# One fused vision block on one core: the experts of two of its four chunks over 512 tokens instead of 256, and several steps moved

## The reference

```
xe = xn * ln_g[e] + ln_b[e]
h  = gelu(xe @ W1[e] + b1[e])      # 64 -> 256
y  = h @ W2[e] + b2[e]             # 256 -> 64
out = sum over the two chosen experts of weight * y
```

## Time and profile before

| | us |
|---|---|
| median of 3 runs (lowest, highest) | 318.96 (318.73, 320.15) |
| the profiled execution | 318.64 |
| its span | 316.9 |
| busy: TensorE, ScalarE, VectorE, GpSimd | 279.8, 256.5, 242.5, 119.8 |
| mean granted clock of TensorE | 0.981 |

### The profile page before, as it was taken

The page is one execution under the profiler, slowest core; times in us unless marked ns, Lnnn a source line. Parts: engine busy times, 40 slices in busy tenths (PEclk is TensorE's granted clock), DMA queues, the critical chain, the costliest instruction groups (busy, mean ns, idle before and its releaser), DMA issues.

```text
span 316.9 us, 8774 instructions
## 1 busy us (share of the span) xinstructions
PE 279.8 (88%) x3434; PEld 191.4 (60%) x3434; DVE 242.5 (77%) x720; ACT 256.5 (81%) x490; POOL 119.8 (38%) x124
## 2 busy tenths in 40 slices
PE   7976998868799898799899999799879999988894
PEld 2552566645467575476577665576667787766462
DVE  6999769799958999659588997586956453589474
ACT  2587678899897999997988899988949898877562
POOL 5040042405142604054466240090836644279130
PEclk9999799989999999999999999999979999999998
DMA  7910000000000000000000000000000000000000
GB/s 157 289 34 0 2 3 4 2 0 0 2 2 4 3 2 2 0 2 8 3 11 2 2 2 0 3 3 8 2 10 2 1 2 2 10 1 11 2 0 17
DMA packets 7190, 4.86 MB, mean 15 GB/s; under 512 B 5089, under 2 KB 6830, under 8 KB 7086
## 3 DMA queue, kind: packets, MB, share of 16 engines
q1 hardware_dynamic: 7150, 4.31, 5.4%
HBM read 2.04 MB, written 0.52 MB: 8 GB/s over the span
## 4 chain that ended last, share of the span: by engine, by line
PE 38%; DVE 27%; ACT 15%; POOL 11%; issue 8%; DMA 1%; SPq 0%; DVEq 0%; ACTq 0%; POOLq 0%
DVE prod L833 4%; PE m_ps L1583 4%; ACT wk L1256 4%; PE zl_ps L1472 4%; PE zh_ps L1469 3%; ACT wk L1251 3%; PE ga_ps L1503 3%; PE ga_ps L1505 3%; PE ga_ps L1504 3%; POOL lx L531 3%; POOL prod L522 3%; PE m_ps L1564 2%; PE m_ps L1566 2%; DVE samp L848 2%; PE m_ps L1447 1%
## 5 line engine op out<-in xcount | busy, mean ns | idle before, releaser
L833 DVE TENSOR_TENSOR prod<-ga_ps,wx 128x480 f32<-128x480 f32 x96 | 61.8, 650 | 36.0 <-PE ga_ps L1505 35.8
L522 POOL TENSOR_TENSOR prod<-prod 128x960 f32<-128x960 f32 (+1 forms) x20 | 39.4, 1969 | 128.2 <-DVE prod L833 128.2
L1503 PE MATMUL ga_ps<-v_all,wk 128*128 128x80 f16 x576 | 80.5, 204 | 6.2 <-DVE prod L833 5.8
L1251 ACT ACTIVATE wk<-zh_ps 128x512 f16<-128x512 f32 x108 | 65.2, 603 | 20.6 <-PE zh_ps L1469 19.5
L1505 PE MATMUL ga_ps<-v_all,wk 128*128 128x80 f16 x576 | 80.5, 204 | 0.0
L1504 PE MATMUL ga_ps<-v_all,wk 128*128 128x80 f16 x576 | 80.5, 204 | 0.0
L1503 PEld LDWEIGHTS ga_ps<-v_all,wk 128*128 128x128 f16 x576 | 57.5, 100 | 18.4 <-issue 9.5
L1256 ACT ACTIVATE wk<-zl_ps 128x512 f16<-128x512 f32 x108 | 65.0, 602 | 0.0
L1504 PEld LDWEIGHTS ga_ps<-v_all,wk 128*128 128x128 f16 x576 | 57.9, 101 | 6.9 <-issue 0.6
L1505 PEld LDWEIGHTS ga_ps<-v_all,wk 128*128 128x128 f16 x576 | 58.1, 101 | 0.0
L1469 PE MATMUL zh_ps<-tab,sel_hi 128*128 128x512 f16 x108 | 42.4, 393 | 6.8 <-ACT wk L1251 5.5
(11 more groups left out here) (278 smaller groups left out, 592.4 us busy)
## 6 DMA issues: line engine op xcount, KB each, us to landing
v_all<-still SPq DMA_DIRECT2D x1, 1440.0 KB, 9.8
h_all<-in_W SPq DMA_DIRECT2D x1, 512.0 KB
w_s<-in_W SPq DMA_DIRECT2D x1, 512.0 KB
x_tok<-in_x SPq DMA_DIRECT2D x1, 384.0 KB, 4.1
out_dram<-x_tok SPq DMA_DIRECT2D x6, 64.0 KB, 1.6
w_high<-w_high SPq DMA_DIRECT2D x1, 256.0 KB, 2.9
const<-in_table SPq DMA_DIRECT2D x1, 218.0 KB, 2.5
vec<-in_vectors SPq DMA_DIRECT2D x1, 132.5 KB
```

The costliest lines, as they stand in the source:

```text
L522: then(pool.tensor_tensor(p[:, 0:3, :], p[:, 0:3, :], p[:, 3:6, :], ALU.add))
L833: dve.tensor_tensor(prod[q % 2][:].rearrange("p k n -> p (k n)")[:, f * PB * NV:(f + 1) * PB * NV] .rearrange("p (n c l) -> p n c l", n=PB ...
L1251: act.activation(wk[n % WR][:, 0, :], zh_ps[:], ACT.Relu, scale=W_SCALE).then_inc(s_wkh, 1)
L1503: pe.matmul(to, w_h, high, start=True, stop=False)
```

## The change

- Experts of chunks 0 and 1 (`d < LAST - 1`): a unit is one half of the hidden layer of one expert over all 512 tokens, two products of 512 columns. `expert_out` works on a pair of experts over 512 columns, four calls instead of eight. `outputs_out` is four copies of 512 columns. Both halves are transposed after all experts are done, the second into `m_ps[0]` and `m_ps[1]`; `input_t` and `samples_t` of later chunks wait for `s_y_rd` for that reason. Chunks 2 and 3 keep the old form.
- `x2` has two buffers, so `residual` waits for the chunk before the last.
- `offsets` signals `s_om` after each bank, `positions` waits for each.
- `input_stats(1)` stands after `hats(0)` instead of before `positions(0)`.
- Products of zeros: two after each of the two first tables, two each at places 19, 19 and 20.5 of the first chunk and at 0 and 3 of the last.
- `outputs_last`: the last 256 tokens by 16 multiply-adds of 64 columns in two chains.
- The tables of places are new. Those that the prediction speaks of are in the diff; others move by a unit or a few.

```diff
 PE_FIRST
-            "bias_product": [0, 0, 0, 3.5, 4.5, 4.5, 5.5, 5.5]}
+            "bias_product": [0, 0, 0, 0, 4.5, 4.5, 5.5, 5.5], "zeros": [19, 20.5, 19]}
...
 PE_MIDDLE
-             "expert_in": [11, 13, 13.5, 14.5, 16.5, 18.5, 19.5, 21, 23, 24, 25.5, 26, 28, 29, 30, 31],
-             "expert_out": [17.5, 19, 20, 23, 27.5, 29.5, 30.5, 32.5], "outputs_t": [25.5, 35.5], "b2": 35}
+             "expert_in": [12, 13, 13.5, 13.5, 16.5, 16.5, 18.5, 18.5, 19.5, 21, 22.5, 23, 24.5, 25, 27, 28],
+             "expert_out": [17.5, 21.5, 26, 31.5], "outputs_t": [32.5, 33], "b2": 35}
...
 ACT_MIDDLE
-              "hidden": [12.5, 12.5, 14.5, 15.5, 18.5, 19, 19.5, 21.5, 24.5, 25, 25.5, 26.5, 28.5, 29.5, 30.5, 31.5],
-              "outputs_out": [23.5, 32.5]}
+              "hidden": [12.5, 12.5, 14.5, 15, 17.5, 18, 18.5, 19.5, 21.5, 22, 22.5, 23.5, 25.5, 26.5, 27.5, 28.5],
+              "outputs_out": [20, 30.5, 30.5, 31.5]}
...
 DVE_MIDDLE
-              "bias_rows": 4.5, "router_parts": 12.5, "w1_low": [8, 9.5, 11, 17], "outputs_in": [23.5, 35]}
+              "router_parts": 12.5, "w1_low": [8, 9.5, 11, 17], "outputs_in": [31.5, 33]}
-POOL_MIDDLE = {"tap_tree": [16.5, 22.5, 25.5, 34.5], "combine": [27, 35.5], "conv_rstd": 21, "inner_rstd": 14,
+POOL_MIDDLE = {"tap_tree": [18.5, 21, 23.5, 35.5], "combine": [35, 35.5], "conv_rstd": 19, "inner_rstd": 12,
...
-POOL_LAST = {"tap_tree": [4, 19.5, 21.5, 35, 42.5, 53.5, 66.5, 71.5], "combine": [37, 53.5], "conv_rstd": 30.5,
-             "inner_rstd": 2.5, "input_rstd": 47, "half_inner_rstd": 44.5, "router_exp": 17.5, "half_router_exp": 71}
+POOL_LAST = {"tap_tree": [4, 21.5, 30.5, 35, 44.5, 55.5, 68, 71.5], "combine": [32.5, 58.5], "conv_rstd": 30.5,
+             "inner_rstd": 0.5, "input_rstd": 47, "half_inner_rstd": 45.5, "router_exp": 25, "half_router_exp": 69.5}
...
@@ positions
-                dve.wait_ge(s_om, a + 1)
-                for t in range(TP):
+                for bank in range(2):
+                    dve.wait_ge(s_om, 2 * a + bank + 1)
+                    for t in range(2 * bank, 2 * bank + 2):
...
@@ outputs_last
+                acc = [seen["wexp"]] * 2
+                parts = [(m_ps[2], m_ps[3], 0, 4), (z_ps[0][:, 0:P], z_ps[0][:, P:2 * P], 4, 2), (ga_ps[0][:, 0:P], ga_ps[0][:, P:2 * P], 6, 2)]
+                for part, (left, right, e0, count) in enumerate(parts):
+                    dve.wait_ge(s_yt, 2 * d + 3 + part)
+                    for e in range(count):
+                        for t, bank in enumerate((left, right)):
+                            dve.wait_ge(s_chain, acc[t])
+                            first, final = e0 + e == 0, e0 + e == E - 1
+                            ins = dve.scalar_tensor_tensor(
+                                out_s[:, d * TP + 2 + t, :] if final else ysum[:, t, :], bank[:, e * C:(e + 1) * C],
+                                wexp[:, 2 + t, e0 + e:e0 + e + 1], x2(d)[:, 2 + t, :] if first else ysum[:, t, :], ALU.mult, ALU.add)
...
@@ vector, start
-            input_stats(1)
             positions(0)
...
             hats(0)
+            dve.wait_ge(s_x_rest, N_X)
+            input_stats(1)
             tap_weights(0)
@@ expert_in
+                if d < LAST - 1:
+                    c0 = n * P
+                    pe.matmul(m_ps[n % 2], w1_high[:, c0:c0 + P], zn_both[:], start=True, stop=False)
+                    pe.matmul(m_ps[n % 2], w1_low[:, c0:c0 + P], zn_high[:], start=False, stop=True).then_inc(s_h, 1)
+                    return
@@ expert_out
+                pe.wait_ge(s_ht, d * (2 * E) + 4 * m + 4)
+                if m == 0:
+                    pe.wait_ge(s_es, min(d + 3, CHUNKS))
+                    pe.wait_ge(s_y_rd, 2 * d)
+                else:
+                    pe.wait_ge(s_ysb, copies_before(d) + m - 1)
+                for a in range(HC):
+                    for r in range(2):
+                        ins = pe.matmul(m_ps[2 + m % 2][r * C:(r + 1) * C, :], w2_s[:, (2 * m + r) * HC + a, :],
+                                        h_t[(4 * m + 2 * r + a) % HR].rearrange("p a n -> p (a n)"), start=(a == 0), stop=(a == HC - 1))
@@ tensor, start
             for r in range(2):
                 features_t(0, r)
+                keep_clock(ga_ps[0][:], FILL[6])
```

More of the change, by code:

```diff
@@ new lines @@
+ACT_FIRST = {"pad_image": 4, "project_high": 8.5, "image_out": 10.5, "conv_gelu": 14.5, "tap_exp": 19.5, "distances": 22.5,
+             "samples_out": 6, "zn_out": 17, "router_exp": 8,
+             "hidden": [4.5, 15.5, 26.5, 34, 34.5, 39, 46.5, 51, 60, 61, 63, 69.5, 69.5, 70, 70.5, 78],
+             "outputs_out": [31.5, 31]}
+DVE_FIRST = {"input_stats": 15.5, "input_norm": 29.5, "input_low": 3.5, "conv_stats": 10, "project_low": 7.5,
+             "conv_norm": 13, "image_out": 13, "positions": [15, 17.5, 15], "rows": [17.5, 17.5, 17.5, 22], "edges": 20.5,
+             "hats": 23.5, "tap_weights": [24.5, 26], "lane_sum": [9.5, 9.5, 17.5, 17.5, 28, 29, 3, 4.5], "residual": 4.5,
+             "inner_norm": 12, "zn_low": 2, "route": [4, 13, 14.5], "expert_weights": 14.5, "b2": 18.5, "bias_rows": 4,
+             "router_parts": 2.5, "w1_low": [7, 8, 14, 26.5], "outputs_in": [17.5, 9.5], "second_stats_": 4,
+             "second_norm": 0.5}
@@ new lines @@
+POOL_FIRST = {"tap_tree": [4, 7, 23.5, 28.5], "combine": [35.5, 22.5], "conv_rstd": 4, "inner_rstd": 21.5,
+              "input_rstd": 26.5}
+PE_MIDDLE = {"input_t": 0, "convolve": [4, 6, 6, 7], "project": 5, "image_t": [9, 12.5], "conv_t": 14.5, "offsets": 15.5,
+             "table": [34, 35.5], "samples_t": 3, "project_out": 4, "experts_t": 8, "router": 11.5,
+             "expert_in": [12, 13, 13.5, 13.5, 16.5, 16.5, 18.5, 18.5, 19.5, 21, 22.5, 23, 24.5, 25, 27, 28],
+             "expert_out": [17.5, 21.5, 26, 31.5], "outputs_t": [32.5, 33], "b2": 35}
@@ L910, in inner_norm @@
                 dve.wait_ge(s_y_r, d + 1 + (half or 0))
[L911 removed]
+                normalise(zn, x2(d), y_mv, y_r[:, 0, :], s_zn, half)
             def logit_scale(d, half=None):
@@ L1351, in body @@
                                 hidden(j - 1, u)
+                        for m in range(E // 2):
+                            if j < LAST and n == at["outputs_out"][m]:
+                                outputs_out(j - 1, m)
                         for i in range(2):
-                            if n == at["outputs_out"][i]:
-                                outputs_out(j - 1, i)
+                            if j == LAST and n == at["outputs_out"][i]:
+                                outputs_out_half(LAST - 1, i)
             act.wait_ge(s_wa, N_WA)
@@ L1574, in expert_out @@
                 if m == 0:
-                    pe.wait_ge(s_es, chunks)
-                    if d == LAST:
-                        pe.wait_ge(s_y_rd, 2 * d)
-                if 2 * m == E and d < CHUNKS - 1:
+                    pe.wait_ge(s_es, CHUNKS)
+                    pe.wait_ge(s_y_rd, 2 * d)
+                if 2 * m == E and d < LAST:
                     pe.wait_ge(s_y_rd, 2 * d + 1)
```

202 lines of the change are left out of this document (104 added, 98 removed).

## The result

The changed kernel takes 322.52 us (median of 4 runs, 320.18 to 324.41) against 318.85 for the kernel before in the same comparison: ratio 1.0121, 95% interval 1.0073 to 1.0170. It is slower by 1.2%. The forecast was 314.7 us and faster, with a chance of 0.77, and its range ended at 318.5. What came is in the main rival (b), which had 0.09: the end of a chunk. The profiled execution took 321.14 us, its span 319.4, at a mean granted clock of 0.989.

The account below looks back on a forecast made before the run. No engine was full; ScalarE and TensorE, handing work over through single banks, were taken to bound it. Terms -0.6 - 0.9 - 0.8 - 1.0 - 0.7 = -4.0 from 318.64 gave 314.7 us on balance, range 311.0 to 318.5.

Parts of the forecast that it names:

- rival (b): Chunk ends: combine ahead of the last tap sum delays the next chunk, 3 us per boundary, 320.7 us; chance 0.09.
- Start-up, -0.6: Before the first tables: moving the moments and signalling offsets by bank together save 0.6 us.
- the cap: First chunk's start: column weights come 0.4 us later, hidden unless TensorE is much earlier; limits the first chunk's gain.
- First chunk, -0.9: First chunk: avoided clock falls gain 1.2 and 0.1 us, uncovered zero products cost 0.4.
- The fall at 31.8: First chunk: TensorE's half clock for 3.4 us vanishes with chance 0.65, helped by four zero products; 1.2 us gained.
- Middle chunks, -0.8: Second and third chunk: 512-token form saves 0.7 us each, longer blocks cost 0.3; net 0.4 each.
- Rival (a): Middle chunks: long bare blocks and end transposes turn the gain into +0.9 us a chunk, 317.3 us; chance 0.20.
- Last chunk, -1.0: Last chunk: GpSimd's power behind the tap sum saves 0.7 us; the clock fall 0.5 less 0.2 for zero products.
- The wait of 3.21 us: Last chunk: VectorE idles behind GpSimd's power and tap sum; removing this gains 0.7 us.
- The fall at 233.2: Last chunk: lowered TensorE clock loses about 1.0 us; even odds that zero products remove it, counted as 0.5.
- Tail, -0.7: End of kernel: last sums as 16 multiply-adds in two chains, 0.20 us apart, finish 0.7 us earlier.
- Rival (c): First and last chunk: zero products catch no clock fall, gains of 1.2 and 0.5 go, 316.4 us; chance 0.12.

Follow-up runs that it names:

- e9_best: e6_before_first with the moments ahead of the positions again, as in the kernel before; 316.21 us, ratio 0.9952.
- e1_two_yb: The changed kernel with two buffers yb instead of one; 324.51 us, ratio 1.0197.
- e8_start_tail: The kernel before with three edits: moments behind the hats, offsets signalled by bank, last sums as multiply-adds; 317.23 us, ratio 0.9971.
- e4_tail_only: The kernel before with only the last sums as 16 multiply-adds; 317.97 us, ratio 0.9978.
- e6_before_first: Changed kernel with two yb, both combines behind the last tap sum, first-chunk tables of before, no zero products in start-up and first chunk; 317.66 us, ratio 0.9980.
- e10_last_tables: e9_best with the last chunk's tables of before and no zero products in that chunk; 315.86 us, ratio 0.9942.
- e7_no_zeros: Changed kernel with two yb and both combines behind the last tap sum, without any new zero products; 319.57 us, ratio 1.0024.
- e3_all_but_512: Kernel before with the change's start-up edits, first-chunk tables, their zero products and last sums, without the 512-token form; 319.52 us, ratio 1.0016.
- e11_block_later: e9_best with the first second-layer block of the middle chunks at place 19 instead of 17.5; 322.45 us, ratio 1.0146.
- e5_order_alone: The changed kernel with its single yb, both combines moved behind the last tap sum; 335.42 us, ratio 1.0535.

## Why the prediction was wrong, point by point

The step that failed is the one put as rival (b): "GpSimd takes the first combine in front of the last tap sum". It was seen, its chain was named and 3 us a boundary was its price, but it got 0.09 where it should have led. The sum put the boundary at nothing. It cost 3.8 us in all: after against e9_best, the difference goes from +0.2 at 1/34 to +3.4 at 2/3, is +3.0 at 3/0, and reaches +4.0 at 3/71 (the first boundary 2.8, the second 1.0). Two things in it were misjudged.

- **The argument against it read a row wrongly.** The tap sum's 3.57 us was taken as a sign of slack. It is a conflict: it started at 155.20, 0.16 behind VectorE's `wx` (the last row below, all of the kernel before), and without a `wx` beside it the same addition takes 2.21 us (158.19 in the rows above), 1.36 less. In the changed kernel it is the combine that starts beside `wx` and takes 2.61 for 1.27, 1.34 more. So the conflict did not go with the new order, it moved to the combine, and what was counted as slack was never given back. The Trainium skill, "SBUF — State Buffer", section "SBUF: two separate sides", says that a VectorE operation with two inputs in SBUF and a GpSimd operation that reads SBUF exclude each other: who starts first holds the shared ports for the whole instruction, and the other is blocked. The traces agree: `wx` reads two tiles in SBUF, starts at 153.58, the combine at 153.75, when 1.48 us of `wx` are left, and the excess is 1.34. They show the other direction too, where GpSimd is in front: VectorE's instruction at 75.67 ends only with the addition that began at 74.54, after 1.72 us, where it takes 0.18 at 31.01.

```profile
31.01 0.18 DVE L804 TENSOR_SCALAR esn<-esum 128x32 f32<-128x32 f32 x1
...
74.54 2.81 POOL L522 TENSOR_TENSOR prod<-prod 128x960 f32<-128x960 f32 x1 [11.46 <-DVE prod L833]
...
75.67 1.72 DVE L804 TENSOR_SCALAR esn<-esum 128x32 f32<-128x32 f32 x1
...
155.04 1.65 DVE L821 TENSOR_TENSOR wx<-dl,mask 128x1440 f32<-128x1440 f32 x1
```

- **The chain had one more link.** I let the loss begin with the tap sum. In fact the first wait is VectorE's for the single `yb` (2.56 us), since the products of both halves now start 6.0 us apart (152.39 and 158.36, the wait included), where the kernel before has 19.7 between them (139.24 and 158.93). The tap sum was the next in line, as e1_two_yb shows with 2.78 us.

The terms of the sum:

- **Start-up, -0.6: the first table was earlier, the end was not.** The first unit came 0.6 us earlier, as put. But the cap that the prediction named (0.4 us of column weights, hidden "as long as TensorE is not much earlier") was the path itself: 0.4 us slower in the traces and 0.6 at full clock with the moved moments (e8_start_tail against e4_tail_only, e6_before_first with 316.58 against e9_best with 315.92 to 316.05). The row at 35.78 was misread: it is VectorE's `weigh`, and it has no wait in front. VectorE's own queue was full up to it, and with `wx` 0.4 us later it comes 0.4 later. The sign was wrong. Offsets by bank were never run alone.

```profile
35.58 0.16 DVE L893 SCALAR_TENSOR_TENSOR w_r_low<-aff,w_r_high 64x8 f16<-64x8 f32 x1
35.78 0.66 DVE L833 TENSOR_TENSOR prod<-ga_ps,wx 128x480 f32<-128x480 f32 x1
```

- **First chunk, -0.9: not a property of the order.** The fall at 31.8 was gone in the profile and unit 4 came 1.8 us earlier. But e9_best and e10_last_tables run the same program up to the last chunk, and one has the fall at 31.8 and the other not; it costs 1.1 us (38.6 for 37.5), where 1.2 was forecast. The second one, at 69.4 in the same trace, costs nothing (1.2 apart at 0/16, 1.2 at 1/0), where 0.1 was. So the size of this fall was right, and the claim that four zero products govern it was not: e7_no_zeros. The new tables make falls near 55 and later in the chunk more frequent, for 1.9 us in the median.
- **Middle chunks, -0.8: right, once the boundary is repaired.** e10_last_tables against e4_tail_only, which differ in the 512-token form with its buffers and tables and in the offsets by bank: 315.64 to 315.88 (four executions at a clock of 0.994 to 0.995) against 316.5 to 316.7, 0.8 us. The traces place half of it elsewhere: e10_last_tables takes 136.5 us from 1/0 to 3/0 for 136.9 before (the second chunk 0.7 less, the third 0.3 more), and 62.5 from 3/0 to 3/71 for 62.9 in e3_all_but_512 and e8_start_tail, which like it have the tables of before and no fall there. Why the last chunk gains wasn't tested, so that the sum was met is in part luck. A block takes 1.94 us (1.88 forecast). Two copies take 1.26 with one of 0.69, a pitch of 0.57 (0.58 forecast; 0.61 by the formula of the Trainium skill, "ScalarE: Activation LUTs", which stands in its section "What ACT_TABLE_LOAD costs"). Two first-layer products are 0.22 apart. Rival (a), bare blocks, is refuted in its general form, since the two chunks together do not grow; but e11_block_later shows its mechanism, with the clock's part in it, at 3 us a chunk when one is moved off its cover.

```profile
146.38 1.26 ACT L1322 ACTIVATE y_sb<-m_ps,b_col 128x512 f32<-128x512 f32 x2
...
149.30 0.69 ACT L1322 ACTIVATE y_sb<-m_ps,b_col 128x512 f32<-128x512 f32 x1 [0.68 <-PE m_ps L1621]
```

- **Last chunk, -1.0: nothing.** The wait of 3.21 us did go, and e10_last_tables, which has it again, is 0.35 us faster. It was covered: from 3/0 to 3/71 the new tables take 62.4 us (e6_before_first) and those of before 62.5 (e10_last_tables), both without a fall, and behind 3/71 the new ones lose 0.3. A wait counts only where it ends last; I should have asked TensorE and ScalarE at 250 us, not VectorE. The fall at 233.2, put at about 1.0 us, costs 0.1: 63.0 before, 62.9 in e3_all_but_512 and e8_start_tail without it.
- **Tail, -0.7: right.** The sums run from 314.04 to 317.21, 3.17 us for the forecast 3.2, at a distance of 0.19 to 0.20. At full clock the part is worth 0.9.

```profile
314.43 1.23 DVE L1035 SCALAR_TENSOR_TENSOR ysum<-m_ps,wexp,ysum 128x64 f32<-128x64 f32 x6
...
316.74 0.47 DVE L1035 SCALAR_TENSOR_TENSOR x_tok<-ga_ps,wexp,ysum 128x64 f32<-128x64 f32 x2
```

So the middle chunks and the tail were worth -1.5 and are worth about -1.7; the start, the first and the last chunk were put at -2.5 and are worth nothing or a loss; the boundary was put at 0 and costs 3.8. Rival (c) was right that the zero products catch no fall, but it kept the other terms.

What isn't settled: why the clock falls in one execution and not in the next at the same place of the same program, and which of the last chunk's moved places costs the 0.3 us in the tail. That the excess of GpSimd's instructions is a lock is argued from durations and the Trainium skill; no run took `wx` alone away from beside the combine, so its share of the 3.8 us isn't measured.

## What to carry to other kernels

When two steps that used to be half a stage apart are moved next to each other, list for each buffer between them who must read it before the next write, and walk the in-order queues at that place with real durations, before counting what the step itself saves: the saving here was 0.8 us, the hand-over cost 3.8. A wait found in the trace is no gain until the engine that sets the end is shown to wait with it; a duration longer than its twins of the same shape may be a conflict with another engine, as here, and not slack. And a repair that makes things worse alone (e1_two_yb, e5_order_alone) may be half of the right one.

## What the runs showed of the hardware that was not expected

- The same program has a mean granted clock between 0.98 and 1.0 from execution to execution, and the time follows in steps, though not in the order of that mean: e9_best takes 315.9 to 316.3 at 0.988 to 1.0, 317.0 to 317.3 at 0.995 and 317.9 to 318.0 at 0.984. What a fall of 3.4 us costs depends on its place: 1.1 us at 31.8 (e10_last_tables against e9_best), 1.0 near 238 (e9_best against e6_before_first: 0.4 us ahead at 3/0, 0.6 behind at 3/71), 0.1 at 233.2, nothing at 69.4, and 1.6 at 133.0 in e8_start_tail, which is 0.2 us ahead of before at 1/18 and 1.4 behind at 1/34, with the same places in that chunk. The Trainium skill, "TensorE: Matmul & The Clock Gate", section "Terms", puts the penalty at half of the lowered time, 1.7 us for 3.4; the runs here show 0 to 1.6. TensorE is busy for 3.0 to 3.4 of the 3.4 us in all five, so that alone does not tell the cost.

```profile
133.00:136.40 3.40, 3.30 (x14) 1.35 (x13) 0.13 (x1) 1.98 (x5) 0.00 (x0) 0.51 0.00 0
```

- GpSimd's additions take 1.34 to 1.37 us longer when they start 0.16 to 0.17 us behind a `wx` of VectorE of 1.65 us (2.61 for 1.27, 3.57 and 3.58 for 2.21; before, after, e3_all_but_512 and e8_start_tail). Beside the 0.90 us instruction at 74.38, of which 0.74 were left, it is 0.60 (2.81 at 74.54). Both times the excess is 0.12 to 0.15 less than what was left.
